# Channel mix as one unrolled pipeline, a reordered opening of relative attention, and 64-line products with a new engine order in mLSTM

## The chip, the cores and the metric

One core of one Trainium2 chip runs the whole program. The metric is the time of one execution on the device in microseconds, the median of several runs. Nothing is exchanged with another core.

## The reference

Six layers follow one another on x (8 batches, 256 tokens, 256 features, float32). Each adds its result to x and normalises the rows: retention with a gated feed-forward part, cross attention on a context, channel mix, attention with relative positions, an mLSTM cell, and a product-key expert layer. The change touches three of them, which compute:

```
# channel mix
xr = mu_r * x + (1.0 - mu_r) * x_prev;  xk = mu_k * x + (1.0 - mu_k) * x_prev
out = sigmoid(xr @ W_r.T) * (square(relu(xk @ W_k.T)) @ W_v.T)
# relative attention, 16 heads of 16, distances clipped to 64
score = q @ k.T + q . pe_k[dist];  ctx = softmax(score) @ v + attn . pe_v[dist]
# mLSTM, 4 heads of 64
log_D = cs[t] - cs_shift[s] + ig[s]  (s <= t);  D = exp(log_D - max_log_D)
C = (q @ k.T / 8) * D;  h = C / max(|sum C|, exp(-max_log_D)) @ v;  then a layer norm per head
```

x_prev is x shifted by one token. dist is the clipped difference of two positions, and pe_k and pe_v are looked up by it.

## The kernel before

The program is written by hand, engine by engine, and each layer is a block of its own: all five queues leave one block before the next begins, and x goes through DRAM between two layers. Order comes from the order in which each engine's code is written and from semaphores. There are eight banks of PSUM, shared by all layers. `turn` (L84) transposes a batch of 256 tokens with four matmuls against the identity, `project` (L92) and `by_token` (L99) are the two forms of a 256 x 256 product (each of 4 matmuls of 256 columns per batch, which run as 8 passes), `row_stats` (L119) and `normalise` (L130) are the layer norm on VectorE.

**Channel mix** (`channel_mix_layer`, L1039) is a hardware loop of four turns on every engine, each turn taking two batches. TensorE turns both batches, waits for `mixed`, makes the k and r products of each (banks 4u+2 and 4u+1) and then both v products (bank 4u+3). ScalarE copies the transposed batch out (`shifted`, L1092), scales it four times into `before` (L1099), and later makes relu (L1104) and sigmoid (L1106). VectorE makes `mixed` (four instructions per batch, L1117), `k_act` (L1125), `y` (L1130, L1132), the statistics and the normalised output. GpSimd makes the inverse square root. The next two batches are loaded into the same two `xin` buffers when `y` has been made.

**Relative attention** (`relative_attention_layer`, L1158) is already unrolled: steps s run from -5, and for each unit U (4 heads of a batch, 32 units) a table of products with the distance embeddings (`table`, L1569) goes to DRAM and comes back skewed as `bias`, while `scores` (L1550), the exponentials, the transposes of the probabilities and the value products follow in later steps. Ahead of the steps stands an opening: SyncE issues 22 loads of constants and weights besides the batches, GpSimd clears `qr`, `probs`, `bias`, `v` and `band_v`, waits for all the loads, and makes small constants up to `const_in` (L1340). TensorE waits for that, multiplies `const_in` by `wo` (L1522), VectorE adds `bo` (L1434), and only then does TensorE turn the first batch.

**mLSTM** (`mlstm_layer`, L1672) works in units of two heads of a batch (16 units). Per unit TensorE makes in this order: `distances(s+1)`: a product of the lines `minus` and `m` (L1990, 32 lines of the array for each of the two heads, 384 columns) and the mask (L1994, 128 lines); `products(s)` = q times k (L1979, 64 lines for each head); `outputs(s-1)` (L2005 to L2007, 128 lines, 65 columns). ScalarE makes the exponentials `decay` (L1845) and, once per batch, the square `sq` (L1836) of the centred result, and in a step that has both the square stands first in its queue:

```
if (b := norm_of(s)) is not None:
    act.wait_ge(cen_ready, b + 1)
    nc.scalar.activation(sq[:, b % 2], hn[:, b % 2], ACT.Square).then_inc(sq_ready, 1)
if (U := unit(s + 1)) is not None:
```

VectorE multiplies both into `c` (L1897) and, once per batch, normalises (L1915 to L1934, then L1938, L1903, L132), with GpSimd making roots and the output `y`.

## Time and profile before

| | us |
|---|---|
| median of 3 runs | 2080.76 (2073.78 to 2081.3) |
| the profiled execution | 2090.12 |
| its span | 2088.3 |
| channel mix, first load to last normalised row | 642.3 to 744.7 |
| relative attention, first load to last store issued | 748.3 to 1211.4 |
| mLSTM, first load to last store issued | 1214.7 to 1381.5 |
| TensorE busy, of the span | 1691.1 (81%) |
| VectorE busy | 1280.4 (61%) |
| mean granted TensorE clock | 0.895 of 2.4 GHz |

A row of the timeline gives the start, the duration, the engine, the line, the tile written and the tiles read, the number of instructions merged into the row, and in brackets how long the engine had been idle and what ended that. PE is TensorE's matmul row and PEld its weight load. PEclk is the clock that TensorE was granted, 1.00 being 2.4 GHz and 0.50 being 1.2 GHz. SPq, DVE, ACT and POOL are SyncE's queue, VectorE, ScalarE and GpSimd.

### The profile page before, as it was taken

How to read it: one execution, taken by the hardware profiler on the slowest of the kernel's cores; microseconds unless marked ns; L12 is line 12 of the kernel's file. 1: busy time of each engine (PE TensorE's matmuls, PEld its weight loads, DVE VectorE, ACT ScalarE, POOL GpSimd, SP SyncE). 2: the span in 40 equal slices, each digit the busy share in tenths (PEclk: the TensorE clock that was granted, in tenths of full speed). 3: DMA queues.
4: the chain of work that ended last, by engine and by line, in shares of the span. 5: the costliest groups of instructions: out<-in, count | busy, mean ns of one | idle time of the engine just before them, and what ended most of it. 6: DMA issues, size and time to landing. Idle time of an engine off the chain costs nothing. (4 is left out here: it accounts for less than half of the span.)

```text
span 2088.3 us, 34248 instructions
## 1 busy us (share of the span) xinstructions
PE 1691.1 (81%) x12550; PEld 1307.3 (63%) x12550; DVE 1280.4 (61%) x3839; ACT 684.5 (33%) x1444; POOL 291.6 (14%) x244
## 2 busy tenths in 40 slices
PE   5798987489984637888888769849799999999987
PEld 4676765356653525666666646648577777777766
DVE  3556544145533413555565525644899999999995
ACT  3323321145552314555555412102322222222210
POOL 1433433100000030000000002321010010010010
PEclk9999998689996677999999966569999999999999
DMA  3000000201001127988888660053000000000000
GB/s 110 6 11 22 6 6 11 77 17 32 13 12 57 40 68 263 331 294 296 293 298 309 217 158 6 21 192 133 1 1 11 1 11 11 1 11 11 1 6 11
DMA packets 97221, 176.17 MB, mean 84 GB/s; under 512 B 16484, under 2 KB 81508, under 8 KB 92260
## 3 DMA queue, kind: packets, MB, share of 16 engines
q1 hardware_dynamic: 97060, 174.02, 24.0%
q8 instruction: 101, 1.65, 0.3%
q14 instruction: 60, 0.49, 0.1%
HBM read 94.17 MB, written 79.69 MB: 83 GB/s over the span
## 5 line engine op out<-in xcount | busy, mean ns | idle before, releaser
L2511 PE MATMUL bank<-per_up,per_act_w 128*128 128x256 f32 x1024 | 246.7, 386 | 22.0 <-DVE per_yout L2402 11.9
L95 PE MATMUL bank<-per_xT,per_down 128*128 128x256 f32 x1024 | 256.2, 396 | 2.3 <-ACT per_xT L2209 1.6
L2511 PEld LDWEIGHTS bank<-per_up,per_act_w 128*128 128x128 f32 x1024 | 194.4, 192 | 52.8 <-DVE per_act_w L2392 27.1
L95 PEld LDWEIGHTS bank<-per_xT,per_down 128*128 128x128 f32 x1024 | 189.2, 194 | 25.6 <-issue 2.7
L2216 ACT ACTIVATE per_act_w<-bank 128x512 f32<-128x512 f32 x128 | 76.2, 597 | 352.0 <-PE bank L95 306.3
L2381 DVE TENSOR_TENSOR per_hot_x<-per_picksT,per_iota_x 128x4096 f16<-128x4096 f16 x64 | 155.8, 2434 | 0.0
L1444 DVE CUSTOM_DVE_ANT_0 rel_summed<-bank,rel_bias 128x256 f32<-128x256 f32 x256 | 93.1, 423 | 61.6 <-PE bank L1550 48.6
L1362 ACT ACTIVATE rel_probs<-rel_summed,rel_low 128x256 f32<-128x256 f32 x256 | 114.1, 519 | 10.6 <-DVE rel_low L1444 10.6
L95 PE MATMUL bank<-ret_x2T,ret_w_in 128*128 128x256 f32 x384 | 98.2, 416 | 15.3 <-DVE ret_x2T L437 15.3
L2498 PEld LDWEIGHTS bank<-per_hot_y,per_hot_x 128*128 128x128 f16 x2048 | 68.6, 96 | 62.5 <-issue 48.6
L870 DVE TENSOR_REDUCE xat_mx<-bank 128x2 f32<-128x512 f32 x128 | 79.5, 684 | 44.9 <-PE bank L914 44.8
L2498 PE MATMUL bank<-per_hot_y,per_hot_x 128*128 128x32 f16 x2048 | 71.2, 177 | 34.1 <-DVE per_act_w L2392 34.1
L95 PEld LDWEIGHTS bank<-ret_x2T,ret_w_in 128*128 128x128 f32 x384 | 78.8, 210 | 30.2 <-DVE ret_x2T L437 16.7
L2392 DVE TENSOR_TENSOR per_act_w<-bank,per_act_w 128x512 f32<-128x512 f32 x128 | 88.0, 691 | 12.3 <-PE bank L2498 2.0
L2195 POOL TENSOR_TENSOR per_sim<-per_sim,per_best_i 128x512 f32<-128x512 f32 x32 | 44.3, 1407 | 365.8 <-DVE per_sim L2331 365.8
L1582 PE MATMUL bank<-rel_ident,rel_probs 128*128 128x128 f32 x512 | 85.5, 315 | 0.8 <-DVE rel_pT L1453 0.5
L1582 PEld LDWEIGHTS bank<-rel_ident,rel_probs 128*128 128x128 f32 x512 | 71.8, 211 | 21.5 <-issue 21.1
L1370 ACT ACTIVATE rel_pT<-bank 128x512 f32<-128x512 f32 x64 | 38.2, 597 | 142.7 <-PE bank L1582 142.6
L1550 PE MATMUL bank<-rel_kT,rel_qT 32*128 32x256 f32 x512 | 55.5, 469 | 27.5 <-issue 9.8
L1594 PE MATMUL bank<-rel_ident,rel_by_dist 128*128 128x128 f32 x256 | 47.8, 311 | 33.7 <-DVE rel_wT L1512 33.7
L842 ACT ACTIVATE xat_probs<-bank 128x512 f32<-128x512 f32 x128 | 66.2, 612 | 12.5 <-PE bank L930 12.5
L1594 PEld LDWEIGHTS bank<-rel_ident,rel_by_dist 128*128 128x128 f32 x256 | 36.0, 208 | 45.3 <-issue 45.3
(350 smaller groups left out, 3287.4 us busy)
## 6 DMA issues: line engine op xcount, KB each, us to landing
rel_qr_rows<-rel_qr SPq DMA_DIRECT2D x32, 1024.0 KB, 6.8
rel_p_rows<-rel_probs SPq DMA_DIRECT2D x32, 1024.0 KB, 4.7
rel_bias<-rel_qr_rows SPq DMA_DIRECT2D x64, 384.0 KB, 4.2
rel_by_dist<-rel_p_rows SPq DMA_DIRECT2D x64, 384.0 KB, 4.8
per_down<-in_per_down SPq DMA_DIRECT2D x1, 4096.0 KB, 25.4
per_up<-in_per_up SPq DMA_DIRECT2D x1, 4096.0 KB, 13.5
ret_xin<-in_x SPq DMA_DIRECT2D x8, 256.0 KB, 2.8
x_after_ret<-ret_yout SPq DMA_DIRECT2D x8, 256.0 KB, 2.1
```

Source lines behind the costliest of these rows:

```text
L95: last = pe.matmul(dst, wt[:, c], src[:, c, :], start=c == 0, stop=c == DC - 1)
L842: nc.scalar.activation(probs[:, U % 2, r], tiles(second_bank(U, r)), ACT.Exp)\
L870: dve.tensor_reduce(mx[:, b % 2, :, 4 * (U % GROUPS) + r], tiles(first_bank(U, r)), AX.X, ALU.max).then_inc(max_taken, 1)
L1362: last = nc.scalar.activation(probs[:, U % 2, r // 2, at:at + SEQ, r % 2], summed[:, r, t], ACT.Exp, bias=low[:, r, t:t + 1], scale=-1.0)
L1444: last = dve.tensor_tensor_reduce(summed[:, r, t], tiles(bank[r])[:, t], bias[:, U % 2, t, r // 2, :, r % 2], 1.0, 3.0e38, ALU.add, ALU.mi ...
L1582: last = pe.transpose(bank[4 + r % 2][:, (2 * c + t) * P:(2 * c + t) * P + P], probs[:, U % 2, r // 2, at:at + P, r % 2], ident[:])
L1594: last = pe.transpose(bank[6][:, (2 * e + t) * P:(2 * e + t) * P + P], by_dist[:, U % 3, t, k, first:first + P, e], ident[:])
L2216: nc.scalar.activation(act_w[:, m % 2, 2 * k:2 * k + 2, :], tiles(bank[3 + k % 2]), ACT.Gelu_apprx_tanh).then_inc(gelu_ready, 1)
L2381: dve.tensor_tensor(hot_x[:, slot].rearrange("p s (c e) -> p s c e", e=4), four(0, wide_x), pattern(iota_x, wide_x), ALU.is_equal)
L2392: dve.tensor_tensor(g, bank[5 + k % 2][:].rearrange("p (s j) -> p j s", j=COLS), g, ALU.mult)\
L2498: last = pe.matmul(bank[5 + u % 2][:, s * COLS:s * COLS + COLS], hot_x[:, slot, at], hot_y[:, slot, at], start=True, stop=True)
L2511: last = pe.matmul(tiles(bank[7])[:, t, :], act_w[:, n % 2, k, t * P:t * P + P], up[:, k, :], start=k == 0, stop=k == COLS - 1)
```

## The change

Channel mix loses its loop: steps s run from -2 to nb, and every engine is written out for one batch per part of a step. In step s TensorE makes the k and r products of batch s, turns batch s+2 and makes the v product of batch s, with banks alternating by batch. VectorE makes `y` of s-1, `k_act` of s, `mixed` of s+1 and the output of s-1. There are four `xin` buffers, and the first batch, the identity and `mu` are loaded ahead of the weights, each with a semaphore of its own.

The opening of relative attention: what were eight loads of `reach_k`, four of `near_v`, two of `base_v` and one of `own` are laid out on the host and come in three loads and as two more columns of `cols`. Only four loads stand ahead of the first projection besides the batch and the identity. The clearing goes from GpSimd to VectorE and covers only the parts that are never written. The constant product goes behind the first table (`constants`), into bank 7.

mLSTM: `m` is copied to all 128 partitions and `minus` has 128 rows, so that the product of lines takes 64 lines of the array per head, half of them zero in `minus`. `products` stands ahead of `distances`, and the exponentials ahead of the square.

```diff
+    XS = 4
...
+    STEPS = range(-2, nb + 1)
...
+            sp.dma_start(xin[:, 0], batch_of(x_in, 0)).then_inc(x_loaded[0], 16)
+            sp.dma_start(ident[:], ident_in).then_inc(ident_loaded, 16)
+            sp.dma_start(mu[:], w["mu"]).then_inc(mu_loaded, 16)
+            sp.dma_start(xin[:, 1], batch_of(x_in, 1)).then_inc(x_loaded[1], 16)
+            weights = load_all(sp, weights_loaded, [(wk[:], w["wk"]), (wr[:], w["wr"]), (wv[:], w["wv"])])
+            for b in range(2, XS):
+                sp.dma_start(xin[:, b], batch_of(x_in, b)).then_inc(x_loaded[b], 16)
...
+            for s in STEPS:
+                if (b := batch(s)) is not None:
+                    act.wait_ge(k_mm, b + 1)
+                    if b >= 2:
+                        act.wait_ge(k_act_ready, b - 1)
+                    nc.scalar.activation(relu_k[:, b % 2], tiles(k_bank(b)), ACT.Relu).then_inc(relu_ready, 1)
+                    act.wait_ge(r_mm, b + 1)
+                    if b >= 2:
+                        act.wait_ge(gated_ready, b - 1)
+                    nc.scalar.activation(r[:, b % 2], tiles(r_bank(b)), ACT.Sigmoid).then_inc(r_ready, 1)
+                if (b := batch(s + 2)) is not None:
+                    act.wait_ge(turned, b + 1)
+                    if b >= 2:
+                        act.wait_ge(mixed_ready, b - 1)
+                    nc.scalar.activation(shifted[:, b % 2, :, 1:SEQ + 1], tiles(turn_bank(b)), ACT.Copy)\
                         .then_inc(xT_ready, 1)
+                    act.wait_ge(xT_ready, b + 1)
                     for k in range(2):
                         for c in range(DC):
+                            last = nc.scalar.activation(before[:, b % 2, k, c, :], shifted[:, b % 2, c, 0:SEQ],
+                                                        ACT.Copy, scale=mu_rest[:, 2 * k + c:2 * k + c + 1])
                     last.then_inc(before_ready, 1)
...
+            for s in STEPS:
+                if (b := batch(s - 1)) is not None:
+                    dve.wait_ge(r_ready, b + 1)
+                    dve.wait_ge(v_mm, b + 1)
+                    dve.tensor_tensor(y[:, b % 2], tiles(v_bank(b)), r[:, b % 2], ALU.mult).then_inc(gated_ready, 1)
+                    dve.drain()
+                    dve.tensor_tensor(y[:, b % 2], y[:, b % 2], xin[:, b % XS], ALU.add).then_inc(x_used, 1)
+                    dve.drain()
+                    row_stats(dve, y[:, b % 2], st, mv[:, b % 2], ve[:, b % 2]).then_inc(var, 1)
+                if (b := batch(s)) is not None:
+                    dve.wait_ge(relu_ready, b + 1)
+                    if b >= 2:
+                        dve.wait_ge(v_mm, b - 1)
+                    dve.scalar_tensor_tensor(out=k_act[:, b % 2], in0=tiles(k_bank(b)), scalar=0.0,
+                                             in1=relu_k[:, b % 2], op0=ALU.max, op1=ALU.mult)\
+                        .then_inc(k_act_ready, 1)
+                if (b := batch(s + 1)) is not None:
+                    dve.wait_ge(before_ready, b + 1)
+                    if b >= 2:
+                        dve.wait_ge(r_mm, b - 1)
                     for k in range(2):
                         for c in range(DC):
                             last = dve.scalar_tensor_tensor(
+                                out=mixed[:, b % 2, k, c, :], in0=shifted[:, b % 2, c, 1:SEQ + 1],
+                                scalar=mu[:, 2 * k + c:2 * k + c + 1], in1=before[:, b % 2, k, c, :],
                                 op0=ALU.mult, op1=ALU.add)
                     last.then_inc(mixed_ready, 1)
+                if (b := batch(s - 1)) is not None:
+                    dve.wait_ge(rstd, b + 1)
+                    if b >= 2:
+                        dve.wait_ge(stored[b % 2], 16 * (b // 2))
+                    normalise(dve, yout[:, b % 2], y[:, b % 2], mv[:, b % 2], rs[:, b % 2])[-1].then_inc(y_ready, 1)
...
+            pe.wait_ge(ident_loaded, 16)
+            for s in STEPS:
+                if (b := batch(s)) is not None:
+                    if b == 0:
+                        pe.wait_ge(weights_loaded, 16 * 3)
+                    pe.wait_ge(mixed_ready, b + 1)
+                    if b >= 2:
+                        pe.wait_ge(k_act_ready, b - 1)
                     for g in range(DC):
+                        last = project(pe, tiles(k_bank(b))[:, g], wk[:, :, g * P:g * P + P], mixed[:, b % 2, 1])
                     last.then_inc(k_mm, 1)
+                    if b >= 2:
+                        pe.wait_ge(r_ready, b - 1)
+                    by_token(pe, tiles(r_bank(b)), mixed[:, b % 2, 0], wr).then_inc(r_mm, 1)
+                if (b := batch(s + 2)) is not None:
+                    pe.wait_ge(x_loaded[b % XS], 16 * (b // XS + 1))
+                    if b >= 2:
+                        pe.wait_ge(xT_ready, b - 1)
+                    turn(pe, tiles(turn_bank(b)), xin[:, b % XS], ident).then_inc(turned, 1)
+                if (b := batch(s)) is not None:
+                    pe.wait_ge(k_act_ready, b + 1)
+                    if b >= 2:
+                        pe.wait_ge(gated_ready, b - 1)
+                    by_token(pe, tiles(v_bank(b)), k_act[:, b % 2], wv).then_inc(v_mm, 1)
...
+    loads = [(cols[:], w["cols"]), (wq[:], w["wq"]), (wk[:], w["wk"]), (reach_k[:], w["reach_k"])]
+    late_loads = [(near_v[:], w["near_v"]), (base_v[:], w["base_v"].partition_broadcast(P)),
+                  (bo[:], w["bo"].partition_broadcast(P)), (wo[:], w["wo"])]
...
-            for b in range(2):
-                sp.dma_start(xin[:, b], batch_of(x_in, b)).then_inc(x_loaded[b], 16)
+            sp.dma_start(xin[:, 0], batch_of(x_in, 0)).then_inc(x_loaded[0], 16)
+            sp.dma_start(ident[:], ident_in).then_inc(ident_loaded, 16)
             load_all(sp, loaded, loads)
-            for b in range(2, XS):
+            sp.dma_start(wv[:], w["wv"]).then_inc(wv_loaded, 16)
+            load_all(sp, late, late_loads)
+            for b in range(1, XS):
...
-            pool.memset(qr[:], 0.0)
-            pool.memset(probs[:], 0.0)
-            pool.memset(bias[:], 0.0)
-            pool.memset(v[:], 1.0)
             pool.memset(band_v[:], 0.0)
             pool.wait_ge(loaded, 16 * len(loads))
-            pool.tensor_scalar(minus_own[:], own[:], -SCALE, None, ALU.mult)
+            pool.tensor_scalar(minus_own[:], own, -SCALE, None, ALU.mult)
             pool.drain()
-            pool.tensor_tensor(bq_own[:], bq.unsqueeze(1).broadcast_to([P, 2, DC]), over(minus_own[:], DC), ALU.mult)
+            pool.tensor_tensor(bq_own[:], bq.unsqueeze(1).broadcast_to([P, 2, DC]), over(minus_own[:], DC), ALU.mult)\
+                .then_inc(bq_ready, 1)
             for t, far in ((0, 2 * P - 2), (1, 0)):
-                pool.tensor_scalar(band_k[:, t], reach_k[:, REACH * t:REACH * t + BAND], reach_k[:, far:far + 1], None,
-                                   ALU.subtract)
+                last = pool.tensor_scalar(band_k[:, t], reach_k[:, REACH * t:REACH * t + BAND],
+                                          reach_k[:, far:far + 1], None, ALU.subtract)
+            last.then_inc(band_ready, 1)
+            pool.wait_ge(late, 16 * len(late_loads))
             pool.tensor_tensor(band_v[:, :, 0:HD], near_v[:], base_v[:], ALU.subtract)
-            pool.drain()
             for t in range(TT):
                 last = pool.tensor_scalar(const_in[:, t], over(bv, P), far_v[:, t:t + 1], None, ALU.add)
-            last.then_inc(consts, 1)
+            last.then_inc(const_in_ready, 1)
...
-            dve.wait_ge(const_mm, 1)
-            dve.tensor_tensor(const_row[:], tiles(bank[0]), bo[:].unsqueeze(1).broadcast_to([P, TT, D]), ALU.add)\
-                .then_inc(const_ready, 1)
+            dve.memset(qr[:, :, :, BAND:BAND + P], 0.0)
+            dve.memset(qr[:, :, :, 2 * BAND + P:ROW], 0.0)
+            dve.memset(v[:, :, :, :, HD:VW], 1.0)
+            dve.memset(bias[:, :, 0, :, NEAR:SEQ], 0.0)
+            dve.memset(bias[:, :, 1, :, 0:REACH], 0.0)
+            dve.memset(probs[:, :, :, SEQ:WIDE - SEQ], 0.0)
+            dve.drain()
...
+                if table_of(s) == 0:
+                    dve.wait_ge(late, 16 * len(late_loads))
+                    dve.wait_ge(const_mm, 1)
+                    dve.tensor_tensor(const_row[:], tiles(bank[7]), bo[:].unsqueeze(1).broadcast_to([P, TT, D]),
+                                      ALU.add).then_inc(const_ready, 1)
 
         @block.tensor
         def _(pe):
-            pe.wait_ge(loaded, 16 * len(loads))
-            pe.wait_ge(consts, 1)
-            for t in range(TT):
-                for c in range(DC):
-                    last = pe.matmul(tiles(bank[0])[:, t], const_in[:, t, c], wo[:, c], start=c == 0, stop=c == DC - 1)
-            last.then_inc(const_mm, 1)
-            pe.wait_ge(const_ready, 1)
+            pe.wait_ge(ident_loaded, 16)
+
+            def constants():
+                pe.wait_ge(late, 16 * len(late_loads))
+                pe.wait_ge(const_in_ready, 1)
+                for t in range(TT):
+                    for c in range(DC):
+                        last = pe.matmul(tiles(bank[7])[:, t], const_in[:, t, c], wo[:, c], start=c == 0,
+                                         stop=c == DC - 1)
+                last.then_inc(const_mm, 1)
...
                     table(U, s)
+                    if U == 0:
+                        constants()
...
-                if (b := norm_of(s)) is not None:
-                    act.wait_ge(cen_ready, b + 1)
-                    nc.scalar.activation(sq[:, b % 2], hn[:, b % 2], ACT.Square).then_inc(sq_ready, 1)
...
                     last.then_inc(decay_ready, 1)
+                if (b := norm_of(s)) is not None:
+                    act.wait_ge(cen_ready, b + 1)
+                    nc.scalar.activation(sq[:, b % 2], hn[:, b % 2], ACT.Square).then_inc(sq_ready, 1)
...
-            dve.tensor_copy(m[:, SEQ:SPAN], m[:, P:SEQ]).then_inc(m_ready, 1)
+            dve.tensor_tensor(top[:], csum[:, 1:SEQ + 1], m[0:LINES, 0:SEQ], ALU.add).then_inc(top_ready, 1)
+            dve.tensor_copy(m[0:LINES, SEQ:SPAN], m[0:LINES, P:SEQ])
+            dve.drain()
...
-                    copy = slice(R * k, R * k + R)
+                    copy = slice(LINES * k, LINES * k + LINES)
...
+                if (U := unit(s)) is not None and U >= 1:
+                    products(U)
                 if (U := unit(s + 1)) is not None:
                     distances(U)
-                if (U := unit(s)) is not None and U >= 1:
-                    products(U)
                 if (U := unit(s - 1)) is not None:
                     outputs(U)
...
-    minus = np.zeros((2 * lines, lines, P), np.float32)
-    minus[np.arange(2 * lines), np.arange(2 * lines) % lines] = -1.0
+    minus = np.zeros((2, P // 2, lines, P), np.float32)
+    minus[:, np.arange(lines), np.arange(lines)] = -1.0
+    minus = minus.reshape(P, lines, P)
```

The rest of the diff takes the host arrays over to the new layouts, and splits the semaphores.

TensorE in channel mix. Before, one turn of the loop (two batches), with the sequencer's rows of the loop:

```order
L88 MATMUL bank<-mix_ident,mix_xin 128x128 x8
L1148 ISA
L95 MATMUL bank<-mix_mixed,mix_wk 128x256 x4
L103 MATMUL bank<-mix_wr,mix_mixed 128x256 x4
L1148 REGISTER_ALU
L95 MATMUL bank<-mix_mixed,mix_wk 128x256 x4
L103 MATMUL bank<-mix_wr,mix_mixed 128x256 x4
L103 MATMUL bank<-mix_wv,mix_k_act 128x256 x8
```

Now, from the start of the layer:

```order
L88 MATMUL bank<-mix_ident,mix_xin 128x128 x8
L95 MATMUL bank<-mix_mixed,mix_wk 128x256 x4
L103 MATMUL bank<-mix_wr,mix_mixed 128x256 x4
L88 MATMUL bank<-mix_ident,mix_xin 128x128 x4
L103 MATMUL bank<-mix_wv,mix_k_act 128x256 x4
L95 MATMUL bank<-mix_mixed,mix_wk 128x256 x4
L103 MATMUL bank<-mix_wr,mix_mixed 128x256 x4
```

The turning of a later batch now stands between the r and the v product of every batch.

VectorE in channel mix now, one batch in the middle of the layer (`mix_y` first of batch s-1, `mix_mixed` of s+1); before, each of these groups stood for two batches in turn:

```order
L1151 TENSOR_TENSOR mix_y<-bank,mix_r 128x512
L1153 TENSOR_TENSOR mix_y<-mix_y,mix_xin 128x512
L122 BN_STATS mix_st<-mix_y 128x6 x2
L125 BN_AGGR mix_mv<-mix_st 128x2 x2
L127 TENSOR_SCALAR mix_ve<-mix_mv 128x2
L1160 SCALAR_TENSOR_TENSOR mix_k_act<-bank,mix_relu_k 128x512
L1169 SCALAR_TENSOR_TENSOR mix_mixed<-mix_shifted,mix_mu,mix_before 128x256 x4
L132 TENSOR_SCALAR mix_yout<-mix_y,mix_mv,mix_rs 128x256 x2
```

The output of a batch now stands behind the mixing of the batch after the next.

TensorE in mLSTM, from the middle of the layer, before (one unit and the start of the next):

```order
L1990 MATMUL bank<-mls_m,mls_minus 128x384 x2
L1994 MATMUL bank<-mls_mask,mls_ident 128x2x128 x2
L1979 MATMUL bank<-mls_xT,mls_cT 128x256 x2
L1979 MATMUL bank<-mls_xT,mls_cT 128x128 x2
L2005 MATMUL bank<-mls_v,mls_c 128x65
L2006 MATMUL bank<-mls_v,mls_c 128x65
```

and now:

```order
L2047 MATMUL bank<-mls_xT,mls_cT 128x256 x2
L2047 MATMUL bank<-mls_xT,mls_cT 128x128 x2
L2058 MATMUL bank<-mls_m,mls_minus 128x384 x2
L2062 MATMUL bank<-mls_mask,mls_ident 128x2x128 x2
L2073 MATMUL bank<-mls_v,mls_c 128x65
L2074 MATMUL bank<-mls_v,mls_c 128x65
```

The two products with 64 lines now follow one another, and so do the two kinds with 128.

## Rows read from the trace of the kernel before

**Rows 1.** Windows view: stretch, length, busy of each engine, PEclk, DMA share, GB/s
```profile
642.00:748.00 106.00, 61.21 (x224) 49.19 (x224) 44.55 (x112) 37.35 (x64) 7.40 (x11) 0.69 0.14 48
1255.00:1346.70 91.70, 83.68 (x365) 58.02 (x364) 52.64 (x136) 21.35 (x62) 23.97 (x19) 0.65 0.04 12
841.00:1200.00 359.00, 298.96 (x2895) 232.86 (x2893) 211.07 (x734) 196.87 (x446) 12.58 (x13) 0.96 0.82 290
794.00:841.00 47.00, 39.87 (x220) 29.83 (x220) 22.37 (x88) 23.92 (x55) 1.26 (x1) 0.69 0.80 290
```

**Rows 2.** Timeline, last turn of channel mix's loop (two batches)
```profile
722.25 3.29 ACT L1099 ACTIVATE mix_before<-mix_shifted,mix_mu_rest 128x256 f32<-128x256 f32 x8
723.98 3.27 DVE L1117 SCALAR_TENSOR_TENSOR mix_mixed<-mix_shifted,mix_mu,mix_before 128x256 f32<-128x256 f32 x8 [3.17 <-ACT mix_before L1099]
...
735.11 3.43 PEld L103 LDWEIGHTS bank<-mix_wv,mix_k_act 128*128 128x128 f32 x16
...
737.32 0.69 DVE L1130 TENSOR_TENSOR mix_y<-bank,mix_r 128x512 f32<-128x512 f32 x1 [2.20 <-PE bank L103]
...
740.13 0.69 DVE L1130 TENSOR_TENSOR mix_y<-bank,mix_r 128x512 f32<-128x512 f32 x1
...
743.97 0.73 DVE L132 TENSOR_SCALAR mix_yout<-mix_y,mix_mv,mix_rs 128x256 f32<-128x256 f32 x2 [0.27 <-POOL mix_rs L1083]
```

**Rows 3.** Timeline, start of channel mix
```profile
642.30 0.35 SPq L51 DMA_DIRECT2D mix_ident<-in_ident  x1
...
648.67 1.97 PE L88 MATMUL bank<-mix_ident,mix_xin 128*128 128x128 f32 x8 [13.68 <-DMA mix_xin<-x_after_xat]
...
654.62 3.78 PE L95 MATMUL bank<-mix_mixed,mix_wk 128*128 128x256 f32 x8 [3.98 <-DVE mix_mixed L1117]
```

**Rows 4.** DMA view: issue, size, median us from issue to landing
```profile
mix_xin<-x_after_xat SPq DMA_DIRECT2D x8, 256.0 KB, 2.7
```

**Rows 5.** Timeline, opening of relative attention
```profile
748.26 0.90 SPq L1275 DMA_DIRECT2D rel_xin<-x_after_mix  x2
...
748.30 3.51 POOL L1325 MEMSET rel_qr<- 128x4096 f32 x1
...
763.86 0.22 POOL L1331 TENSOR_SCALAR rel_minus_own<-rel_own 128x2 f32<-128x2 f32 x1 [1.60 <-DMA rel_base_v<-in_rel_ext_v]
...
768.31 3.75 PE L1522 MATMUL bank<-rel_wo,rel_const_in 128*128 128x256 f32 x8 [29.37 <-POOL rel_const_in L1340]
...
774.36 1.99 PE L95 MATMUL bank<-rel_xT,rel_wq 128*128 128x256 f32 x8 [0.77 <-ACT rel_xT L1378]
...
780.68 0.93 PE L1569 MATMUL bank<-rel_band_k,rel_qT 32*128 32x191 f32 x16 [0.88 <-DVE rel_v L1466]
...
793.67 0.43 DVE L1444 CUSTOM_DVE_ANT_0 rel_summed<-bank,rel_bias 128x256 f32<-128x256 f32 x1 [9.11 <-DMA rel_bias<-rel_qr_rows]
```

**Rows 6.** Timeline, TensorE over one unit of mLSTM at 1.2 GHz, and the next start
```profile
1308.28 1.65 PE L1990 MATMUL bank<-mls_m,mls_minus 32*128 32x384 f32 x4
...
1309.86 2.08 PE L1994 MATMUL bank<-mls_mask,mls_ident 128*128 128x256 f32 x4
...
1311.86 1.65 PE L1979 MATMUL bank<-mls_xT,mls_cT 64*128 64x256 f32 x8
...
1313.44 0.69 PE L2005 MATMUL bank<-mls_v,mls_c 128*128 128x65 f32 x2
...
1316.19 1.65 PE L1990 MATMUL bank<-mls_m,mls_minus 32*128 32x384 f32 x4
```

**Rows 7.** Timeline, VectorE over one batch of mLSTM, and ScalarE ahead of it
```profile
1298.43 0.63 ACT L1836 ACTIVATE mls_sq<-mls_hn 128x512 f32<-128x512 f32 x1 [12.82 <-DVE mls_hn L1934]
...
1300.34 1.02 DVE L1897 SCALAR_TENSOR_TENSOR mls_c<-bank,mls_decay 128x384 f32<-128x384 f32 x2 [1.94 <-ACT mls_decay L1845]
...
1305.70 1.02 DVE L1897 SCALAR_TENSOR_TENSOR mls_c<-bank,mls_decay 128x384 f32<-128x384 f32 x2 [2.28 <-PE bank L1979]
...
1315.03 1.02 DVE L1897 SCALAR_TENSOR_TENSOR mls_c<-bank,mls_decay 128x384 f32<-128x384 f32 x2 [1.94 <-ACT mls_decay L1845]
```

149 lines of the change are left out of this document (62 added, 87 removed).

## The prediction

> **What bounds the kernel now.** The layers run one after another, so what a change is worth is read stage by stage. I first cut the span into windows [rows 1]. Over channel mix no engine is busy for more than 61.2 of 106.0 us: the stage is bound by waits that follow one another. Its timeline says which [rows 2, 3]: the mixing waits 3.17 us for ScalarE's scaling, the product 3.98 us for the mixing, VectorE 2.20 us for the product, and then everything waits for the next two batches. The opening of relative attention was read in the same view [rows 5]: the first load is issued at 748.26, but TensorE starts at 768.31, after 29.37 us of idling, behind GpSimd, which has cleared tiles and waited for the last small load until 763.86. The first scores are used at 793.67, 45.4 us into the layer. In mLSTM TensorE is busy 83.7 of 91.7 us, at a granted clock of 0.65 [rows 1]. Half a clock is 1.2 GHz, so 0.65 means 70% of the time at the low level, where TensorE has no gap [rows 6]. At the high level VectorE and ScalarE bound it [rows 7].
>
> **Channel mix.** *Work per batch.* At 2.4 GHz a pass of 256 columns takes 3.43/16 = 0.214 us [rows 2]. Three products of 8 passes are 5.14 us, a turn of four 128-column transposes about a third of one product (0.6): 5.7 us of TensorE. VectorE: from one `y` to the next 740.13 - 737.32 = 2.81, the mixing 3.27/2 = 1.64, the output 0.73 [rows 2], and `k_act`, a 128x512 operation like `y`'s, 0.69: 5.9 us. ScalarE: 3.29/2 for scaling and three 128x512 activations, which I put at 0.6 each (the scaling takes 0.41 for 256 columns): 3.5 us. In the new order `y`'s wait is covered: the v product can start when `k_act` is there, 3.5 us into VectorE's batch, and takes 1.7 and the 0.5 that lie between a product's start and its use (735.11 to 737.32 is 2.21), so the next `y` can start at 5.7, just before VectorE is free. GpSimd's root falls behind `k_act` and the mixing, the loads are up to four batches ahead, so both cost nothing while the period is above their 3 us. I take 6.0 us per batch, near VectorE's 5.9; the other end is TensorE always at 1.2 GHz, 11.4.
>
> *Start and end.* Against the first load at 642.30: batch 0 lands after 2.7 [rows 4], its turn takes 1.1 (half of 1.97 and a latency), the copy 0.8, scaling 1.65, mixing 1.75, together 8.0; I add 0.3 for the queues: first product at 650.6 instead of 654.62. By the second turn's start in rows 3 plus its length (650.6) everything now loaded had landed, so the weights are not later. Then the clock is low, as it is before (3.78 us for 8 passes), and rises during batch 0, as it did one batch later before: k, r, turn and v take 9 us, which puts the first `y` at 659.7. Seven periods later, 701.7, the last one begins, and from there to the end it takes the same as before (740.13 to 744.7): 706.3. The gain is 38.4. From it I take 2.0 for stretches at 1.2 GHz, which the dense stage of rows 1 (0.96) also has. **36.4 us**; its ends are 0 (low clock always) and 39.
>
> **Opening of relative attention.** Bytes ahead of the first projection: batch 256 KB, identity 64, wq and wk 512, `reach_k` and `cols` 0.13 MB: 0.97 MB. In channel mix 1.09 MB (identity, three weights, a batch) took 6.4 us, 642.30 to 648.67 [rows 3], so these take 5.7. GpSimd's two small operations 0.6, the copy of the turned batch 0.7: projection at 7.0 instead of 26.1 (774.36 - 748.26). But it now meets a cold TensorE: before, the constant product, 3.75 us from 768.31, had come first. Its 24 passes take 5.1 us at 2.4 GHz and 10.3 at 1.2; the low clock lasts for about half of it, as in batch 0 above, 7.7. Then the 1.2 us that lie between the passes' end and the table (780.68 - 774.36 - 5.1): the table at 15.9 instead of 32.4. The constant product, 8 passes or 1.7 us, is now behind the first table. It delays the second one, whose copy to DRAM waits for the first one's return anyway. From the table to the first use the way through DRAM is the same 13.0 us [rows 5]. VectorE's clearing of 4,600 elements, at GpSimd's 3.51/4096, is 4 us, finished before its first copy is wanted at about 15; it would cost only if it took three times as long. The steps afterwards are unchanged. **16.0 us**, between 13.9 (low clock throughout) and 19.
>
> **mLSTM.** A pass of 384 columns at 1.2 GHz is 0.64 us, of 256 columns 0.43. So the lines' product (two passes per half of the array, both halves at once) streams for 1.28 of its 1.58, the mask for 1.71 of 2.00, the q-k product (768 columns per half) for 1.28 of 1.58 [rows 6]. The 0.3 us at each end stand where the next product uses another number of lines. Of four such changes per unit two vanish: 7.91 becomes about 7.35, 14.7 per batch. Using 64 lines instead of 32 costs no time, since passes are paid by column. At the high clock VectorE's batch counts: 14.69 between two `c` of the same kind, less 2.28 and 1.94 of waits [rows 7], is 10.5; with the exponentials first, the 1.94 (square and exponentials behind one another) are off its path, and I take 10.8. The window of rows 1 holds 13 units (28 TensorE instructions each, 365) in 91.7 us, 7.05 each. With 70% of the time low: 1/(0.70/7.35 + 0.30/5.4) = 6.63, 5.5 us less. Two or three units lie outside (1.5), and the last batch's 1.94 is wholly on the path. **9.0 us**. The ends are -1 (always low: 13 units of 0.3 more, less the rest) and 24 (always high). `minus` doubles from 1 to 2 MB. At the rate above (1.09 MB in 6.4 us) it lands 6 us later; its first use is some 33 us into the layer, behind the whole chain of the gates, so I price it at nothing, and at 3 us were it issued last. The extra copy of `m` lies beside ScalarE's exponential and the transposes that the first `decay` waits for: nothing, or half a microsecond once.
>
> At one place the Trainium skill is against this. The q-k product's 8 weight loads and passes take no more than streaming and the 0.3 [rows 6], so loads within one half of the array are already hidden, and I price the new boundary between the two 64-line products at 0. The Trainium skill (TensorE: Matmul & The Clock Gate, Part 3, packing small matmuls) says that a weight load overlaps a running matmul only if it goes to other rows of the array. By it each boundary would keep an exposed load, here up to the 0.3 us a boundary shows now, and 16 units would lose at most 4.8 of the 9.0.
>
> **Sum.** 36.4 + 16.0 + 9.0 = 61.4: 2090.1 becomes 2028.7 for the profiled execution, which stood 9.4 above the median of the runs. For the median, 2080.8 - 61.4 = **2019.4 us**. What a measurement here can tell from no change is about 0.5%, 10.4 us.
>
> **Rivals.**
> - *Round trips still bind channel mix.* In-order queues meet: if `k_act`, the v product and `y` follow one another without cover, a period is 5.9 + 2.2 + 0.4 = 8.5 and 7 x 2.5 = 17.5 us are lost: 2037. For: TensorE and VectorE are both over 90% loaded. Against: each wait has another batch's work ahead of it. 12%.
> - *The clock stays at 1.2 GHz in channel mix*: 11.4 per batch, 38 us lost, 2057. For: PEclk 0.69 now. Against: the idle comes from waits that go, and the busy stage has 0.96 [rows 1]. 6%.
> - *mLSTM doesn't get what it is said to get*: the changes of lines go on costing, or `distances`, now behind `products`, waits with it for `c`. 2028. 10%.
> - *mLSTM warms up*: less lost between products, clock high throughout, 15 more: 2004. 8%.
> - *Slower*: the unchanged steps of relative attention fall to the low clock. They start 50 us earlier against the throttle, with the same gap for the way through DRAM, after which they ran at 0.69 for 47 us [rows 1]. If the 359 us stayed at 0.69, their 299.0 us of TensorE would grow by 0.96/0.69, 117 us, of which the 60 us of idle take a part; I put the loss at 90: 2109. From about two thirds of that on it outweighs the gain. Against: before, they recovered from the same start. 3%.
>
> The forecast itself (2008 to 2032) has 0.60, other mishaps 0.01. Range: 2002 to 2042, which takes in the two neighbours on either side and leaves out the low clock and the slower case. Faster by over 0.5%: 0.96, within 0.01, slower 0.03.
>
> **What would show it.** Channel mix: `y` every 6.0 us, PEclk above 0.9, one table load of ScalarE in place of eight, the stage some 65 us from first load to last output. Relative attention: turn about 3 us, table about 16, first use of `bias` about 29 us after the first load, and the windows after that as before. mLSTM: at 1.2 GHz 7.35 per unit, no 0.3 us between q-k and lines, VectorE no longer waiting 1.94 for the exponentials. Wrong if a period above 7.5 us, a table later than 19, or a rise in the length of relative attention's unchanged steps appears.

## The result, and the profile after the change

| | before | after |
|---|---|---|
| median of the runs, measured beside each other | 2079.83 us (4 runs) | 1989.66 us (4 runs, 1986.41 to 1993.68) |
| the profiled execution | 2090.12 | 1987.38 |
| its span | 2088.3 | 1985.6 |
| mean granted TensorE clock | 0.895 | 0.928 |

The ratio is 0.9573 with a 95% interval of 0.9544 to 0.9601: 83 to 95 us less, 90.2 by the medians. The sign was forecast rightly, the size was not: the forecast was 61.4 less, and the measured time lies below its range.

Where did the time go? I cut both traces at the same events. The profiled execution of before stood 10.3 above the median in this table and the one of after 2.3 below, so these lengths add up to 12.6 more than the medians show.

| stage | before | after | less | forecast |
|---|---|---|---|---|
| channel mix, first load to last normalised row | 102.4 | 61.1 | 41.3 | 36.4 |
| relative attention, first load to first use of `bias` | 45.4 | 26.4 | 19.0 | 16.0 |
| its unchanged steps, from there to the last store issued | 417.7 | 411.8 | 5.9 | 0 |
| mLSTM, first load to last store issued | 166.8 | 131.2 | 35.6 | 9.0 |

The windows of after that answer to [rows 1] (length, busy time of PE, PEld, DVE, ACT and POOL, PEclk, DMA share, GB/s), for channel mix, the opening, the unchanged steps, and the middle of mLSTM from 8 us behind its first lines' product to its last:

```profile
641.50:702.61 61.11, 50.05 (x224) 42.07 (x224) 43.14 (x112) 28.53 (x57) 5.92 (x11) 0.89 0.24 79
706.10:732.40 26.30, 13.59 (x84) 10.37 (x84) 7.58 (x12) 6.37 (x12) 5.43 (x10) 0.76 0.59 198
732.40:1144.20 411.80, 334.74 (x3124) 259.61 (x3124) 237.92 (x835) 221.66 (x501) 14.53 (x15) 0.95 0.82 287
1188.20:1250.50 62.30, 53.57 (x364) 41.56 (x363) 50.72 (x138) 20.75 (x58) 24.27 (x20) 0.95 0.05 18
```

The last row is the surprise: PEclk is 0.95 where it had been 0.65, with the same number of TensorE instructions (364 against 365 [rows 1]).

**Channel mix.** The timeline at its start and in the middle (columns as in the rows of before), with what was VectorE's 2.20 us wait [rows 2]:

```profile
641.54 0.37 SPq L1089 DMA_DIRECT2D mix_xin<-x_after_xat  x1
...
644.35 1.11 PE L88 MATMUL bank<-mix_ident,mix_xin 128*128 128x128 f32 x4 [10.11 <-DMA mix_ident<-in_ident]
...
649.83 3.75 PE L95 MATMUL bank<-mix_mixed,mix_wk 128*128 128x256 f32 x8 [2.82 <-DVE mix_mixed L1169]
...
658.50 0.69 DVE L1151 TENSOR_TENSOR mix_y<-bank,mix_r 128x512 f32<-128x512 f32 x1 [1.98 <-PE bank L103]
...
664.14 0.69 DVE L1151 TENSOR_TENSOR mix_y<-bank,mix_r 128x512 f32<-128x512 f32 x1
...
669.82 0.69 DVE L1151 TENSOR_TENSOR mix_y<-bank,mix_r 128x512 f32<-128x512 f32 x1
670.60 0.69 DVE L1153 TENSOR_TENSOR mix_y<-mix_y,mix_xin 128x512 f32<-128x512 f32 x1
671.39 0.75 DVE L122 BATCH_NORM_STATS2 mix_st<-mix_y 128x6 f32<-128x256 f32 x2
672.21 0.25 DVE L125 BATCH_NORM_AGGREGATE mix_mv<-mix_st 128x2 f32<-128x6 f32 x2
672.54 0.17 DVE L127 TENSOR_SCALAR mix_ve<-mix_mv 128x2 f32<-128x2 f32 x1
672.65 0.69 DVE L1160 SCALAR_TENSOR_TENSOR mix_k_act<-bank,mix_relu_k 128x512 f32<-128x512 f32 x1
673.26 1.66 DVE L1169 SCALAR_TENSOR_TENSOR mix_mixed<-mix_shifted,mix_mu,mix_before 128x256 f32<-128x256 f32 x4
674.84 0.73 DVE L132 TENSOR_SCALAR mix_yout<-mix_y,mix_mv,mix_rs 128x256 f32<-128x256 f32 x2
675.50 0.69 DVE L1151 TENSOR_TENSOR mix_y<-bank,mix_r 128x512 f32<-128x512 f32 x1
```

The rows of one batch from 669.82 to 675.50 show no bracket: VectorE never waits there. The stage is bound by VectorE, at 5.67 us per batch, and no longer by waits behind one another. The first of the eight batches has its `y` at 658.50 and the last at 698.21; the last normalised row ends at 702.65.

**Opening of relative attention**, to be read against [rows 5]:

```profile
706.06 0.36 SPq L1319 DMA_DIRECT2D rel_xin<-x_after_mix  x1
...
709.07 1.11 PE L88 MATMUL bank<-rel_ident,rel_xin 128*128 128x128 f32 x4 [10.97 <-DMA rel_ident<-in_ident]
...
713.28 3.69 PE L95 MATMUL bank<-rel_xT,rel_wq 128*128 128x256 f32 x8 [3.09 <-ACT rel_xT L1423]
...
721.29 0.93 PE L1627 MATMUL bank<-rel_band_k,rel_qT 32*128 32x191 f32 x16 [0.88 <-DVE rel_v L1514]
...
723.40 0.33 SPq L1364 DMA_DIRECT2D rel_qr_rows<-rel_qr  x1
...
727.26 0.87 SPq L1343 DMA_DIRECT2D rel_bias<-rel_qr_rows  x2
...
732.45 0.42 DVE L1492 CUSTOM_DVE_ANT_0 rel_summed<-bank,rel_bias 128x256 f32<-128x256 f32 x1 [6.31 <-DMA rel_bias<-rel_qr_rows]
```

**mLSTM.** TensorE over one unit at the high clock, and the next start, against [rows 6]:

```profile
1190.35 0.92 PE L2047 MATMUL bank<-mls_xT,mls_cT 64*128 64x256 f32 x8
1191.10 0.81 PE L2058 MATMUL bank<-mls_m,mls_minus 64*128 64x384 f32 x4
1191.85 1.13 PE L2062 MATMUL bank<-mls_mask,mls_ident 128*128 128x256 f32 x4
1192.82 0.33 PE L2073 MATMUL bank<-mls_v,mls_c 128*128 128x65 f32 x2
...
1194.19 0.92 PE L2047 MATMUL bank<-mls_xT,mls_cT 64*128 64x256 f32 x8
```

A unit is 3.84 us here. VectorE over one batch, from one `hn` to the next, against [rows 7]:

```profile
1214.41 0.75 DVE L1995 TENSOR_TENSOR mls_hn<-bank,mls_norm 128x256 f32<-128x256 f32 x2
...
1216.88 1.02 DVE L1965 SCALAR_TENSOR_TENSOR mls_c<-bank,mls_decay 128x384 f32<-128x384 f32 x2
...
1219.91 1.02 DVE L1965 SCALAR_TENSOR_TENSOR mls_c<-bank,mls_decay 128x384 f32<-128x384 f32 x2
...
1224.76 0.75 DVE L1995 TENSOR_TENSOR mls_hn<-bank,mls_norm 128x256 f32<-128x256 f32 x2
```

Both waits of `c` are gone, the 1.94 for the exponentials and the one for the q-k product, and a batch takes 10.35. Nothing in [rows 7] told that the clock would be high here. That is what the experiments are about.

Of the 35.6 us of mLSTM 29.4 lie between the first product of lines and the last (99.7 to 70.3) and 5.8 behind the last (34.0 to 28.2).

### The profile page after: what moved, and what is told of

Its sections match the earlier page's. It is cut to its first block and busy times, and to the rows that moved or that the text cites. A ratio compares the mean times of both kernels' runs of the same rounds, so it can differ in the third digit from the quotient of the medians.

```text
span 1985.6 us, 34173 instructions
## 1 busy us (share of the span) xinstructions
PE 1637.7 (82%) x12550; PEld 1276.3 (64%) x12550; DVE 1281.0 (65%) x3846; ACT 676.8 (34%) x1437; POOL 276.4 (14%) x240
## 5 line engine op out<-in xcount | busy, mean ns | idle before, releaser
L2566 PE MATMUL bank<-per_hot_y,per_hot_x 128*128 128x32 f16 x2048 | 71.1, 177 | 34.1 <-DVE per_act_w L2460 34.1
L95 PEld LDWEIGHTS bank<-ret_x2T,ret_w_in 128*128 128x128 f32 x384 | 76.9, 204 | 29.4 <-DVE ret_x2T L437 16.7
L1606 PE MATMUL bank<-rel_kT,rel_qT 32*128 32x256 f32 x512 | 49.4, 420 | 27.8 <-issue 9.8
L408 DVE TENSOR_TENSOR ret_probs<-bank,ret_seen 128x256 f32<-128x256 f32 x128 | 45.1, 413 | 33.8 <-PE bank L513 33.7
```

Source lines behind the costliest of these rows:

```text
L95: last = pe.matmul(dst, wt[:, c], src[:, c, :], start=c == 0, stop=c == DC - 1)
L2566: last = pe.matmul(bank[5 + u % 2][:, s * COLS:s * COLS + COLS], hot_x[:, slot, at], hot_y[:, slot, at], start=True, stop=True)
```

## The experiments

I had two theories of the excess. *The clock of mLSTM is the change's own*: the new order or the 64 lines bring it up. The rival, *history*: the layers ahead, now dense, hand the clock over high, and mLSTM would gain about 9 us by itself as forecast. Four kernels put one layer of one program into the other, each with the whole layer and its arrays of the host swapped:

```diff
 # e1, e2, e3: the kernel before, with one layer of the change
+channel_mix_layer            # e1
+relative_attention_layer     # e2
+mlstm_layer                  # e3
 # e4: the changed kernel, with mlstm_layer of before
```

**e1, channel mix alone.** 

> The kernel before with the new channel mix alone. Theory (each layer gains by itself, by the comparison of the two traces: first load to last normalised row 102.4 to 61.1 us): 2039 us, 41 less. The step of the forecast was 36.4, which gives 2043. Rival (the layers share a history: a stage that no longer idles also changes the clock of the stage behind it): a gain that differs from 41 by more than 5 us, and a first 100 us of relative attention whose length differs from that of before by the same.

**e2, opening of relative attention alone.** 

> The kernel before with the new opening of relative attention alone. The step of the forecast was 16.0, which gives 2064. Theory (19.0 us come from the opening itself, 45.4 to 26.4 us up to the first use of bias, and the 6 us of the unchanged steps come from where the low clock happened to fall): 2061, and the unchanged steps between 411 and 418 us. Rival (an opening that keeps TensorE busy also spares the unchanged steps low clock): 2055, unchanged steps at 412 again.

**e3, mLSTM alone.** 

> The kernel before with the new mLSTM alone. The step of the forecast was 9.0, which gives 2071. Theory (the new order and the 64 lines themselves bring TensorE's clock in this layer from 0.65 to about 0.9, whatever ran before it): 2045 to 2050, the layer 131 us long from first load to last store, units of 3.9 us at the high clock. Rival (the clock in mLSTM rose because the layers ahead of it changed): the layer at about 158 us, clock 0.65, 2071.

**e4, all but mLSTM.** 

> The changed kernel with mLSTM as it was (channel mix and the opening new). Theory (the gain of mLSTM is its own): 2015 to 2025 us, 25 to 35 more than the changed kernel, the layer 167 us long at a clock of 0.65. Rival (history): mLSTM runs at the high clock here too and the time is below 2000, as the forecast of 9.0 would also give (1999, with the clock low).

| | median us | ratio to before (2079.69) | interval | stage lengths in its trace |
|---|---|---|---|---|
| e1 | 2045.66 | 0.9835 | 0.9779 to 0.9891 | channel mix 61.2, opening 46.0, unchanged steps 416.1, mLSTM 166.8 |
| e2 | 2064.13 | 0.9925 | 0.9893 to 0.9957 | channel mix 100.8, opening 29.5, unchanged steps 416.5, mLSTM 167.2 |
| e3 | 2054.31 | 0.9877 | 0.9826 to 0.9927 | channel mix 102.7, opening 45.0, unchanged steps 413.5, mLSTM 133.4 |
| e4 | 2020.65 | 0.9718 | 0.9662 to 0.9775 | channel mix 61.2, opening 26.1, unchanged steps 416.0, mLSTM 162.0 |

The medians alone could not have decided: the intervals are 13 to 24 us wide. e1 and e3 lie 7 and 4 us above what the first theory expected of them, and their intervals take it in; e2 has 15.9 us from the opening where that theory had 19.0, and its unchanged steps lie where it put them. The lengths of the stages decide. Where nothing of a stage was altered, channel mix repeats within 1.9 us, and the opening within 1.0 behind the same channel mix, but the unchanged steps only within 6. Channel mix is 61.2 with whatever stands around it. The new mLSTM is 133.4 long in e3, behind the old layers, and the old one 162.0 in e4, behind the new ones. So mLSTM gains 33.4 us alone (166.8 to 133.4) and 30.8 behind the new layers (162.0 to 131.2): most of the gain is its own. The old mLSTM was 166.8 to 167.2 long in before, e1 and e2, so up to 5 of the 35.6 us may be history, or chance; one trace of e4 cannot tell. The middle of mLSTM in e3:

```profile
1249.70:1314.60 64.90, 56.64 (x362) 43.70 (x363) 51.48 (x138) 20.70 (x58) 24.18 (x20) 0.89 0.05 17
```

and in e4:

```profile
1191.30:1281.10 89.80, 82.33 (x366) 57.16 (x364) 52.04 (x135) 20.05 (x60) 23.97 (x19) 0.66 0.04 13
```

The opening of relative attention does have a small share of history: 45.4 to 29.5 behind the old channel mix (before, e2), 46.0 to 26.1 behind the new one (e1, e4).

**Which of mLSTM's three edits?** Five kernels go back on one or two of them in the changed kernel.

```diff
 # e5: ScalarE, the square ahead of the exponentials again
+                if (b := norm_of(s)) is not None:
+                    act.wait_ge(cen_ready, b + 1)
+                    nc.scalar.activation(sq[:, b % 2], hn[:, b % 2], ACT.Square).then_inc(sq_ready, 1)
                 if (U := unit(s + 1)) is not None:
...
 # e6: TensorE, distances ahead of products again
-                    products(U)      # then distances(U)
+                    distances(U)     # then products(U)
...
 # e7: 32 lines per head again (minus and m of 64 rows, no copy of m)
-                    copy = slice(LINES * k, LINES * k + LINES)
+                    copy = slice(R * k, R * k + R)
...
 # e8: e5 and e6 together: of the three edits only the 64 lines are left
 # e10: e6 and e7 together: only the exponentials first are left
```

**e5.** 

> The changed kernel with ScalarE's square ahead of the exponentials again. If the order of ScalarE carries the gain: VectorE waits 1.9 us again in each of 8 batches, and the added idle lets the clock fall: 10 to 30 us slower than the changed kernel (2000 to 2020). If it only removes a wait that other work would cover at the high clock: within 3 us of the changed kernel.

**e6.** 

> The changed kernel with TensorE's distances ahead of the products again (64 lines kept, exponentials first). Four changes of lines per unit come back, at 0.2 us each at the high clock and 0.3 at the low one: 16 units by 0.4 to 0.6, 6 to 10 us (1996 to 2000), if the time is all that they cost. If it is the gaps at these changes that keep the clock low, the granted clock in the middle of mLSTM falls to 0.65 and it is 25 to 35 us (2015 to 2025).

**e7.** 

> The changed kernel with 32 lines per head in the product of lines again (products first, exponentials first). The change from 64 to 32 lines comes back, two per unit: 16 by 0.4 to 0.6, 6 to 10 us (1996 to 2000) if only its time counts; below 2 us if the order alone did it. If the clock follows the share of the array that is in use, it falls in mLSTM: 20 to 35 us (2010 to 2025).

**e8.** 

> The changed kernel with both orders of mLSTM as before, and only the 64 lines new. If the lines in use carry the clock: high (0.9), and the time within 12 us of the changed kernel. If the gaps or the order carry it: the clock at 0.65 and 25 to 35 us slower (2015 to 2025), as with the old mLSTM.

**e10.** 

> The changed kernel with 32 lines and TensorE's old order in mLSTM: of its three edits only the exponentials ahead of the square is left. If ScalarE's order is worth 1.9 us in each of 8 batches whatever the clock is: units of mLSTM take 84 us instead of 98, clock 0.65 to 0.75, about 2006 us, as with the 32 lines and products first. If the order of TensorE had its share in that kernel: 90 us or more, and 2012 or more.

**e12, the changed kernel again.** 

> The changed kernel unaltered, beside the two others on the same chip: 1990 us as before, the layer of mLSTM 131 us, its units 70 us at a clock of 0.95. A length of the units above 80 us here would say that the gain of mLSTM is a matter of chance from run to run and not of the change.

The result, with the time from the first lines' product to the last ("units"), the granted clock in the window described above, and the medians of e5 to e8 beside 2084.66 of before, of e10 and e12 beside 2084.58:

| kernel | 64 lines | products first | exponentials first | units us | clock | whole layer us | median us |
|---|---|---|---|---|---|---|---|
| e4 | | | | 97.8 | 0.66 | 162.0 | 2020.65 |
| e8 | yes | | | 88.9 | 0.81 | 154.1 | 2015.65 |
| e10 | | | yes | 81.4 | 0.82 | 143.3 | 2000.23 |
| e5 | yes | yes | | 85.9 | 0.87 | 148.2 | 2005.91 |
| e7 | | yes | yes | 83.9 | 0.75 | 145.4 | 2006.34 |
| e6 | yes | | yes | 69.7 | 1.00 | 133.4 | 1992.24 |
| after; e12 | yes | yes | yes | 70.3; 70.3 | 0.95; 1.00 | 131.2; 131.8 | 1989.66; 1990.00 |

The table is read in pairs that differ in one edit. **Exponentials first**: 97.8 to 81.4, 88.9 to 69.7, 85.9 to 70.3, so 16 to 19 us. **64 lines**: 97.8 to 88.9, 81.4 to 69.7, 83.9 to 70.3, so 9 to 14. **Products first**: 3.0 less, 2.5 more, 0.6 more, and over the whole layer 5.9 less (e8 to e5), 2.1 more (e10 to e7), 2.2 less (e6 to after), so nothing that can be told; behind the last product of lines alone it took 1.8 to 3.2 off in all three pairs, but with products first that product itself stands later in its step. Products first by itself was not run. The medians follow nearly the same order (e5 and e7, and e6 and after, change places by under 3 us), though not each pair is apart beyond its interval: the ratios to before are 0.9718 (e4), 0.9675 (e8), 0.9598 (e10), 0.9629 (e5), 0.9649 (e7), 0.9567 (e6), and 0.9549 (0.9518 to 0.9580) for e12. e8 lies between its two expectations: the lines alone bring the clock to 0.81, but the time stays near that of the old mLSTM, since the wait is still there. e7 also lies between its two, with the clock at 0.75. e10 came out faster than its 84 us of units and its clock of 0.65 to 0.75, which were what the wait alone would give. e12 repeats the length of after, so it is not chance. e6 missed its expectation of 6 to 10 us (it has two changes of lines per unit more than after, not the four more that stand there), and its row says why; the clock was high throughout, and there TensorE is not what a batch waits for:

```profile
1186.00:1247.70 61.70, 53.92 (x360) 39.30 (x360) 50.92 (x134) 18.82 (x54) 23.98 (x19) 1.00 0.05 18
```

The row of e10, which differs from e6 in the lines alone, has 14 us more of busy TensorE for the same number of instructions, since it was slower:

```profile
1191.00:1264.40 73.40, 67.64 (x366) 47.69 (x364) 50.96 (x134) 19.45 (x56) 23.99 (x19) 0.82 0.05 15
```

What ScalarE's order costs is seen in e5 at the high clock, again from one `hn` to the next:

```profile
1208.73 0.76 DVE L1995 TENSOR_TENSOR mls_hn<-bank,mls_norm 128x256 f32<-128x256 f32 x2
...
1213.21 1.02 DVE L1965 SCALAR_TENSOR_TENSOR mls_c<-bank,mls_decay 128x384 f32<-128x384 f32 x2 [1.94 <-ACT mls_decay L1911]
...
1221.12 0.76 DVE L1995 TENSOR_TENSOR mls_hn<-bank,mls_norm 128x256 f32<-128x256 f32 x2
```

12.39 per batch against 10.35: the wait of 1.94 stands on the path of every batch, as soon as TensorE is at 2.4 GHz. Where a whole batch is at 1.2 GHz, TensorE bounds it at 15.8 (twice the 7.91 from 1308.28 to 1316.19 [rows 6]), and the same wait costs nothing. But it is not free in every batch with the clock low: in before, just behind a high stretch, TensorE itself waited for the exponentials at 1.2 GHz:

```profile
1300.36 1.65 PE L1990 MATMUL bank<-mls_m,mls_minus 32*128 32x384 f32 x4 [1.62 <-ACT mls_decay L1845]
```

**In TensorE's old order the lines change the clock alone.** A unit there is equally long with 32 lines and with 64: at 1.2 GHz 7.92 us in e10 (1228.61 to 1236.53) and in e8 (1257.51 to 1265.43), at 2.4 GHz 4.24 in before (1261.65 to 1265.89) and in e6 (1207.28 to 1211.52).

What came before a change of level? In before, between two low stretches, TensorE was granted 2.4 GHz for 6.8 us and was busy 5.19 of it, then fell back and was busy 22.28 of 23.90:

```profile
1290.80:1297.60 6.80, 5.19 (x38) 3.96 (x36) 6.13 (x15) 0.00 (x0) 2.63 (x2) 1.00 0.11 39
1297.60:1321.50 23.90, 22.28 (x80) 14.93 (x78) 13.29 (x36) 6.24 (x18) 7.25 (x6) 0.50 0.04 12
```

In after a high stretch lasted 34.1 us, with TensorE busy 29.56, and the low ones between the high stretches 3.4:

```profile
1184.40:1218.50 34.10, 29.56 (x210) 22.70 (x208) 23.88 (x63) 12.97 (x39) 9.16 (x7) 1.00 0.03 9
```

and e12 ran all of its window at the high level, with 50.79 of 62.30:

```profile
1193.30:1255.60 62.30, 50.79 (x364) 39.58 (x363) 51.94 (x139) 20.75 (x58) 24.27 (x20) 1.00 0.05 18
```

By these three rows the clock fell where TensorE had the larger idle share at the high level, 24% against 13% and 18%, and the 1.94 us wait of each batch would be part of that share. Two other kernels speak against it. e5, which has the wait, stayed at the high level for 20.5 us with TensorE idle for 34% of it, and was low for only 3.4 on either side. e10, which has not, was idle for 8% of a high stretch and was then low for 13.7:

```profile
1205.90:1226.40 20.50, 13.50 (x98) 10.66 (x96) 13.62 (x38) 5.82 (x17) 6.92 (x6) 1.00 0.04 14
1204.00:1227.90 23.90, 21.95 (x148) 16.07 (x147) 19.59 (x55) 6.38 (x18) 9.15 (x7) 1.00 0.04 12
```

So the idle share does not tell when the clock falls, and how the wait moves the clock stays open; that it does is read from the granted clock in three pairs (0.66 to 0.82, 0.81 to 1.00, 0.87 to 0.95). What differs between the kernels in the middle of the layer is how long the clock stays low once it has fallen: 13.7 to 37.5 us in before, e4, e7 and e10, with 32 lines, and 3.4 to 13.6 in e3, e5, e8 and after, with 64 (e1, with the old mLSTM, has 3.5 and 6.8 beside 23.9). It is not the time lost at the changes of lines either: e6 has as many of them per unit (four) as before, and its clock is 1.00. Why the number of lines in use goes with the clock, no run settles. A version with four products of 32 lines side by side, which would have told the lines of one product from the lines in use, was left untried.

**A version beyond both.** If VectorE bounds mLSTM at the high clock, taking work from it must show. e11 lets ScalarE make the output row and GpSimd the shift:

```diff
-                    normalise(dve, yout[:, b % 2], y[:, b % 2], mv[:, b % 2], rs[:, b % 2])[-1].then_inc(y_ready, 1)
...
+                    for t in range(TT):      # on ScalarE, behind the square
+                        last = nc.scalar.activation(yout[:, b % 2, t, :], y[:, b % 2, t, :], ACT.Identity,
+                                                    scale=rs[:, b % 2, t:t + 1], bias=shift[:, b % 2, t:t + 1])
+                    last.then_inc(y_ready, 1)
```

> The changed kernel with mLSTM's output row (y less its mean, times the root; 1.68 us of VectorE per batch) made by ScalarE, GpSimd making the shift. If VectorE's chain bounds mLSTM now, at the high clock: a period per batch of 8.7 instead of 10.4 us, about 12 us less over the units (1978). If the clock is what bounds (low after a change of lines or when TensorE idles more): no gain, or some us lost. If TensorE bounds a batch at 9: 8 us less.

Measured: 1982.99 us, ratio 0.9511 (0.9481 to 0.9541), beside 1990.00 and 0.9549 (0.9518 to 0.9580) for e12 on the same chip. mLSTM was 122.6 long instead of 131.8, its units 63.9 instead of 70.3, and a batch 8.87:

```profile
1219.34 0.76 DVE L2002 TENSOR_TENSOR mls_hn<-bank,mls_norm 128x256 f32<-128x256 f32 x2
...
1222.46 1.07 ACT L1923 ACTIVATE mls_yout<-mls_y,mls_shift,mls_rs 128x256 f32<-128x256 f32 x2
...
1228.21 0.75 DVE L2002 TENSOR_TENSOR mls_hn<-bank,mls_norm 128x256 f32<-128x256 f32 x2
```

The period fell by 1.5 us, nearly the 1.68 that the output row had taken on VectorE in each batch of e12. The bound named is the right one. By the trace this is 9 us, by the medians 7; the intervals of the two ratios overlap, so the gain of the whole is likely and not shown beyond doubt.

## Why the prediction was wrong, step by step

**The step that failed** is in the sum of mLSTM: "With 70% of the time low". I took the share of the low clock from the window before and kept it. It fell from 70% to 10% (granted clock 0.65 to 0.95), through two edits of mLSTM. One is the exponentials first; the other is the 64 lines, which the prediction put at nothing ("Using 64 lines instead of 32 costs no time") and which the runs show to be worth 9 to 14 us (9 and 12 of them with TensorE's old order, where the units kept their length at either level and only the clock changed). With the periods that the runs show (before 15.8 low and 12.39 high, after 10.36 high, and low 14.7 as computed) and the share kept, the 91.7 us of [rows 1] would have become 91.7 x (0.7/15.8 + 0.3/12.39) / (0.7/14.7 + 0.3/10.36), 82 us: 10 less, the size of the forecast term. The window is 62.3. By this estimate the other 20 us of that window are the clock. Outside the window mLSTM gained 6.2, where I had 3.5. The mechanism had been named, in the rival "mLSTM warms up", but with 8% and 15 us beyond the 9, where the layer got 35.6, or 26.6 beyond. Its upper end was too low as well: "24 (always high)" fell short by 12.

**The term within it, "the 1.94 is off its path", was right in place and under-sized in reach.** I counted it through a mean at the low clock's weight, and once for the last batch. At the high clock it is 2.0 us in each batch (12.39 to 10.35), and 16 to 19 us in all. Eight batches by 2.04 are 16.3 as well, so the total alone doesn't show a part of the clock. With the reckoning above, from the units of e4, e8 and e5 (97.8, 88.9, 85.9) and their low shares kept (0.68, 0.38, 0.26), I estimate 7 to 11 us for the wait itself, which leaves 4 to 10 for the clock. The high-clock batch itself was put at 10.8 and is 10.36. The 7.35 per unit at 1.2 GHz was not seen, as no whole unit of the new form ran at that level in the middle of the layer; e7, with one change of lines less than before, took 7.62 (1228.28 to 1235.90).

**The boundary of two 64-line products** was priced at 0 against the Trainium skill (TensorE: Matmul & The Clock Gate, Part 3, packing small matmuls), which says that a weight load overlaps a running matmul only if it goes to other rows of the array. The rows decide. From L2047 to L2058 it is 0.75 us (1190.35 to 1191.10), of which 0.64 is streaming (half of the 1.28 at 1.2 GHz), so 0.11 is left. The boundary of the two 128-line products is no better: 0.97 from L2062 to L2073 for 0.86 of streaming. In e6, where the lines change at every boundary, the next starts lie as follows:

```profile
1207.28 0.92 PE L2047 MATMUL bank<-mls_xT,mls_cT 64*128 64x256 f32 x8
1208.13 0.44 PE L2073 MATMUL bank<-mls_v,mls_c 128*128 128x65 f32 x2
...
1209.62 0.92 PE L2058 MATMUL bank<-mls_m,mls_minus 64*128 64x384 f32 x4
1210.46 1.13 PE L2062 MATMUL bank<-mls_mask,mls_ident 128*128 128x256 f32 x4
1211.52 0.92 PE L2047 MATMUL bank<-mls_xT,mls_cT 64*128 64x256 f32 x8
```

0.21 us is left behind L2047 and 0.20 behind L2058 and L2062. A unit takes 4.24 there against 3.84 in after. So of the exposed load that the page's rule asks for at the new boundary there is 0.11 us at most, and the saving of TensorE's time was 0.40 a unit at 2.4 GHz. Where it came from was not quite as worked out: "the 0.3 us at each end stand where the next product uses another number of lines" doesn't hold at every boundary. L2058 to L2062 still goes from 64 lines to 128 in after, and only 0.11 is left there too (1191.10 to 1191.85); at 1.2 GHz it is 0.14 in after (1240.45 to 1241.87), and 0.16 between the two 64-line products (1239.01 to 1240.45), where every boundary had kept 0.3 before. No run tells the reason. In the end it gained little: at the high clock VectorE bounds the batch, and e6 was as long as after in its units (69.7 and 70.3), 2.2 us longer over the whole layer and 2.6 by the medians, which is within the scatter.

**Channel mix: right in kind, 4.9 too small** (36.4 to 41.3). The first product came 8.3 us after the first load, as worked out, the first `y` at 17.0 instead of 17.4. The period was 5.67 and not 6.0 (2.3 over seven periods): three of the four terms of VectorE's 5.9 were recorded durations, and `k_act`, the mixing and the output each end 0.07 to 0.08 after the next instruction has started, as 1.66 from 673.26 to the next start at 674.84 shows. Inside the fourth term, from `y` to `k_act`, most instructions follow one another with a gap of 0.07 to 0.1 instead. The 2.0 set aside for low clock did not occur; from 655.3 on it was high for 47.8 us. The rest, 0.1, is the end (4.44 us from the last `y` on, against 4.57). One table load of ScalarE in place of eight came as said. The round trips and the low clock, 12% and 6%, did not happen.

**Opening of relative attention: right.** Turn 3.0 (about 3), projection 7.2 (7.0), table 15.2 (15.9) after the first load; alone it gains 15.9 (e2), against 16.0. (The terms given there, a table at 15.9 and 13.0 from it to the first use, come to a gain of 16.5; the prediction doesn't say where the other 0.5 went.) The further 3 came with the new channel mix. Not quite half of it is the table, at 16.6 in e2 with a granted clock of 0.67 over the opening, and at 15.2 in after with 0.76. The other half is in the way of `qr_rows` through DRAM: from its issue to the issue of `bias` it took 5.5 us in before and in e2,

```profile
766.24 0.34 SPq L1314 DMA_DIRECT2D rel_qr_rows<-rel_qr  x1
771.74 0.88 SPq L1293 DMA_DIRECT2D rel_bias<-rel_qr_rows  x2
```

and 3.9 in after and e4, and 3.8 in e1, which has the old opening behind the new channel mix. So it goes with the channel mix ahead. I have no test of the reason. (e1's opening gained nothing by it, 46.0, since its first projection ran at the low clock: 3.78 us for 8 passes, 1.99 in before.)

**The unchanged steps** took 5.9 us less in the profiled execution. Nothing ties this to the change: with the new opening they are 411.6 to 416.9 long in nine other kernels, with the old one 413.5 to 417.7. The slower case, in which they fall to the low clock (3%), did not come about: their clock is 0.92 to 0.95 in all kernels.

**Sum.** 41.3 + 19.0 + 5.9 + 35.6 = 101.8 in the traces; less the 12.6 by which the two profiled executions stood off their medians it is 89.2, and 90.2 was measured. Of the 28.8 missed, mLSTM carries most.

## What to carry to other kernels

Where a stage runs at a low granted clock, price a change at both levels and ask what moves the share between them. Keeping the old share is a forecast of its own, and here it was the weakest one. A wait that costs nothing at the low level, because TensorE is behind anyway, is paid in every batch at the high one: here 1.94 us per batch were worth 16 to 19 us in all, an estimated 4 to 10 of them by the clock. And where runs scatter by half a per cent, read the lengths of single stages beside the total, and look first how well each of them repeats: within 2 us here for channel mix, within 6 for the steps of relative attention.
